# First stage of a state-space block written out as a four-deep pipeline, and its skip term moved to the third stage

## The chip, the cores and the metric

The kernel runs on one core of a Trainium2 chip. Its engines are TensorE (PE in the profile; PEld is its weight load), VectorE (DVE), ScalarE (ACT), GpSimd (POOL) and SyncE (SP, which here only starts transfers). The metric is the device time of one execution in microseconds (us); lower is better.

## The reference, cut to what matters

The input `x` holds 2 x 4096 tokens of 512 numbers. Four layers follow each other, each added to `x`; the change touches only the first one:

```python
xin = layernorm(x)                      # what the layer gets
xn = layernorm(xin) * norm_w + norm_b   # a second norm inside the layer
proj = xn @ x_proj_w.T                  # 128 + 64 + 64 columns
delta, B, C = split(proj)
dt = softplus(delta @ dt_proj_w.T + dt_proj_b)
h = exp(dt * A) * h + dt * B * xn       # a scan over the tokens, 512 x 64 states
y = sum_n h * C
out = (y + xin * D_param) @ out_proj_w.T
```

The skip term is `xin * D_param`: the once-normed input times a row of 512 constants. C is taken from the first 128 tokens of a sequence.

## The kernel before, in words

The 8192 tokens are cut into NCH = 16 chunks of T = 512. P is 128 (partitions), Q = 4 blocks of 128 columns, J = 4 blocks of 128 tokens. The program has five stages, one after the other, each with its own buffers; between two stages all engines and transfers finish. Everything is in 32-bit floats. Every engine runs its own list of instructions in order, and semaphores (`wait_ge`, `then_inc`) hold one behind another. A `Count` is a semaphore whose value encodes chunk and step.

**First stage (`pre_phase`).** For each chunk: load x (SP), statistics and both norms `z` and `zh` (DVE, with a power on POOL for the root), transposes of `zh` and of `z` (PE, `work`, L357), `znt` out of PSUM with scale and bias (ACT, L312), `zt` out of PSUM (DVE, L282), projection with `xp` (PE, L367), copies `dl` and `bc` (DVE), the step sizes with `dtw` (PE, L372), `xb` out of PSUM with a bias (ACT, L315), Abs, Exp and Ln (ACT, L333 to L335), `dt` and `v` (DVE, L293, L294), transposes of `bc` and `v` (PE, `turn_rows`, L381, L387), copies into rows (ACT, L322, L325), and stores of `zt`, `bc`, `dt`, `br` and `vr`. A chunk owns one half of PSUM (four banks of `tp`), which its steps use one after another. `skewed` runs pieces marked 1 for chunk c + 1 and pieces marked 0 for chunk c in one turn. On ACT the order is

```python
skewed(act, NCH, [(1, columns), (0, rows), (1, exponents)])
```

**Scan (`scan_phase`).** For each chunk and each of 128 items (pairs of states by column blocks), PE makes the input u (L602, `inputs`), ACT the decay, DVE the scan (L663), POOL multiplies by C (L489), and PE transposes and adds the product into `y_ps` (L610, `reduce`). An item's `inputs(i)` is followed in PE's list by `reduce(i - 3)`. At item 3 of a chunk PE first waits until ACT has copied the last chunk's y out of PSUM (L528), and then starts y with the skip term: 16 products of `z` with the diagonal `dd` (L622), which take 32 matmul records. Only then come `reduce(0)` and `inputs(4)`.

**Third stage (`mid_phase`).** For each chunk: transposes of y (PE, `turn_y`, L896 with `mid_yr`), the output projection (L890), a sum and a norm (DVE), a second product (L908), its sum and norm, and four projections of the normed rows (L919, L944). The last of these, `values`, has one DVE copy (L817) for each of its four PSUM banks. The orders are

```python
skewed(dve, NCH, [(1, first_sum), (1, second_sum), (0, keys), (1, more_norms), (0, values)])
skewed(pe, NCH, [(1, turn_y), (0, decay), (1, attn_out), ..., (0, values_early), (1, turn_xn), (0, values_late)])
```

so PE's `turn_y` of the next chunk stands right behind `values_late` of this one.

Of the kernel before, what the change touches and what calls it, by code (L numbers as in the profile page):

```python
# [3 lines left out]
ALU = mybir.AluOpType  # L4
# [3 lines left out]
P = 128  # L8
T = 512
# [134 lines left out]
NORM_BOTH = 10  # L144
# [16 lines left out]
def both_norms(dve, cnt, roots, item, root_n, outs, x, mv, ve, r0, rr, tmp, tiles):  # L161

    roots.wait(dve, item, root_n)
    cnt.link(dve, dve.tensor_tensor(tmp, r0, r0, ALU.mult))
    cnt.link(dve, dve.tensor_tensor(tmp, tmp, ve, ALU.mult))
    cnt.link(dve, dve.tensor_scalar(tmp, tmp, -0.5, 1.5, ALU.mult, ALU.add))
    cnt.link(dve, dve.tensor_tensor(rr, r0, tmp, ALU.mult))
    for e in (1, 0):
        for j in range(tiles):
            last = dve.tensor_scalar(outs[e][:, j, :], x[:, j, :], mv[:, j, 0:1], rr[:, e, j:j + 1], ALU.subtract, ALU.mult)  # L170
        cnt.inc(last)


# [6 lines left out]
def pre_phase(nc, NCH, D, x_d, xp_d, dtw_d, nw_d, nb_d, dtb_d, ident_d, dt_s, vr_s, z_s, bc_s, br_s):  # L180

# [3 lines left out]
    J = T // P  # L187
    with ExitStack() as ctx:
# [3 lines left out]
        tp = ps("tp", [P, 2, Q, T])  # L192
        x = sb("x", [P, 2, J, D]); z = sb("z", [P, 2, J, D]); zh = sb("zh", [P, 2, J, D])
        zt = sb("zt", [P, 2, Q, T]); znt = sb("znt", [P, 2, Q, T])
        dl = sb("dl", [P, T]); bc = sb("bc", [P, 2, T])
        xb = sb("xb", [P, 2, Q, T]); ab = sb("ab", [P, 2, Q, T]); dt = sb("dt", [P, 2, Q, T]); v = sb("v", [P, 2, Q, T])
        vr = sb("vr", [P, J, D]); br = sb("br", [P, J, P])
        st = sb("st", [P, J, 6]); mv = sb("mv", [P, J, 2]); ve = sb("ve", [P, 2, J])
        half_neg = sb("half_neg", [P, 2, J]); r0 = sb("r0", [P, 2, J]); rr = sb("rr", [P, 2, J]); tmp = sb("tmp", [P, 2, J])
# [23 lines left out]

        @block.sync
        def _(sp):
            for dst, src in ((xp, xp_d), (dtw, dtw_d), (ident, ident_d), (nw, nw_d), (nb, nb_d), (dtb, dtb_d)):
                sp.dma_start(dst[:], src).then_inc(consts, 16)

            for par in range(2):
                sp.sem_inc(outs[par], 48)  # L230

            def load(c, par, half):

                norm_steps.wait_freed(sp, c)
                sp.dma_start(x[:, par], xv[c]).then_inc(x_in[par], 16)

            def store(c, par, half):

                proj_steps.wait(sp, c, Q + 2)
                sp.dma_start(z_s[c], zt[:, par]).then_inc(outs[par], 16)  # L240
                sp.dma_start(bc_s[c], bc[:, par]).then_inc(outs[par], 16)
                proj_steps.wait(sp, c, Q + 3)
                sp.dma_start(dt_s[c], dt[:, par]).then_inc(outs[par], 16)
            staggered(sp, NCH, [(2, load), (0, store)])
            for par in range(2):
                sp.wait_ge(outs[par], 48 * (NCH // 2 + 1))

        @block.gpsimd
        def _(pool):
# [3 lines left out]

            def roots(c, par, half):
                root_steps.begin(c)
                root_pool(pool, root_steps, norm_steps, c, BOTH_VE, r0[:], ve[:], half_neg[:])
            in_turn(pool, NCH, roots)

        @block.vector
        def _(dve):  # L260
            norm_steps.start(dve)
            proj_steps.start(dve)

            def stats(c, par, half):
                norm_steps.begin(c)
                dve.wait_ge(x_in[par], (half + 1) * 16)
                both_stats(dve, ticks_dve, norm_steps, x[:, par], st, mv, ve, J)

            def norms(c, par, half):

                pe_steps.wait_freed(dve, c)
                both_norms(dve, norm_steps, root_steps, c, 1, (z[:, par], zh[:, par]), x[:, par], mv, ve[:], r0[:], rr[:], tmp[:], J)

            def turned(c, par, half):
                proj_steps.begin(c)

                dve.wait_ge(outs[par], (half + 1) * 48)

                row_turns.wait_freed(dve, c)
                pe_steps.wait(dve, c, 2)  # L280
                for q in range(Q):
                    proj_steps.inc(dve.tensor_copy(zt[:, par, q, :], tp[:, par, q, :]))  # L282

            def copies(c, par, half):
                pe_steps.wait(dve, c, 3)
                proj_steps.inc(dve.tensor_copy(dl[:], tp[:, par, 0, :]))
                pe_steps.wait(dve, c, 4)
                proj_steps.inc(dve.tensor_copy(bc[:, par, :], tp[:, par, 1, :]))
# [1487 lines left out]
```

## Time and profile before

| what | us |
|---|---|
| median of 3 runs (lowest, highest) | 8550.32 (8546.56, 8552.54) |
| the profiled execution, its own time | 8550.57 |
| its span, first to last instruction | 8548.7 |
| first stage | 0 to 578.6 |
| scan | 578.6 to 5455.7 |
| third stage | 5455.7 to 6962.3 |
| fourth and fifth stage | 6962.3 to 8548.7 |

A row of a timeline gives the start, the length and what ran; equal neighbours are merged (x16), and the bracket at its end is the time for which the engine sat idle before. The stage bounds are the first start of a transfer of the next stage's constants.

### The profile page before, as it was taken

What the parts mean: (1) busy time and instruction counts of PE and PEld (TensorE: products, weight loads), DVE (VectorE), ACT (ScalarE), POOL (GpSimd) and SP (SyncE); (2) the same over time, 40 slices, a digit from 0 to 9 for tenths busy, and PEclk for the clock granted to TensorE, in tenths of its full rate; (3) what the DMA queues carried; (4) which work ended last, traced back from release to release, by engine and by line L of the source; (5) the groups of instructions that cost most, each with busy time, mean ns of one, the idle gap of its engine ahead of it and who ended that gap; (6) DMA issues with size and microseconds to landing.
All of it is one profiled execution on the core that took longest, in us unless ns stands there. A gap on an engine that the chain in (4) does not pass through costs nothing. (4 is left out here: it accounts for less than half of the span.)

```text
span 8548.7 us, 222310 instructions
## 1 busy us (share of the span) xinstructions
PE 7615.9 (89%) x76550; PEld 5597.7 (65%) x76550; DVE 6621.9 (77%) x8318; ACT 4693.7 (55%) x10584; POOL 5667.3 (66%) x3272
## 2 busy tenths in 40 slices
PE   5669999999999999999999999799999989999984
PEld 3347777777777777777777777544444446666653
DVE  4459999999999999999999999522222247787866
ACT  4457777777777777777787777411111112222220
POOL 0019999999999999999999999500000025545444
PEclk8779999999999999999999999999999988888885
DMA  3350000000000000000000000112212122222225
GB/s 130 138 157 9 21 21 1 20 21 20 0 21 21 0 21 21 15 6 21 21 0 21 21 0 5 75 69 88 83 69 88 74 89 77 76 76 78 75 67 168
DMA packets 198856, 423.21 MB, mean 50 GB/s; under 512 B 22544, under 2 KB 48592, under 8 KB 183120
## 3 DMA queue, kind: packets, MB, share of 16 engines
q1 hardware_dynamic: 172864, 382.77, 13.4%
q10 hardware_dynamic: 25872, 38.80, 1.3%
q8 instruction: 80, 1.31, 0.1%
q14 instruction: 40, 0.33, 0.0%
HBM read 225.11 MB, written 196.41 MB: 49 GB/s over the span
## 5 line engine op out<-in xcount | busy, mean ns | idle before, releaser
L489 POOL TENSOR_TENSOR scan_hc<-scan_h,scan_cb 128x1024 f32<-128x1024 f32 x2048 | 4775.4, 2367 | 165.4 <-DVE scan_h L663 96.7
L663 DVE TENSOR_TENSOR_SCAN scan_h<-scan_a,scan_carry,scan_u 128x512 f32<-128x512 f32 x4096 | 4800.3, 1255 | 56.1 <-POOL scan_hc L489 48.8
L548 ACT ACTIVATE scan_a<-scan_dt,scan_aneg 128x512 f32<-128x512 f32 x4096 | 2658.1, 708 | 7.3 <-ACT scan_yo L528 7.3
L602 PE MATMUL scan_u<-scan_dg,scan_v 64*128 64x128 f32 x32768 | 2379.8, 285 | 308.7 <-DVE scan_h L663 265.1
L602 PEld LDWEIGHTS scan_u<-scan_dg,scan_v 64*128 64x128 f32 x32768 | 1990.4, 187 | 786.8 <-DVE scan_h L663 549.5
L610 PE MATMUL scan_y<-scan_ident,scan_hc 128*128 128x128 f32 x16408 | 2239.9, 279 | 7.0 <-POOL scan_hc L489 3.1
L610 PEld LDWEIGHTS scan_y<-scan_ident,scan_hc 128*128 128x128 f32 x16408 | 1756.9, 140 | 256.3 <-POOL scan_hc L489 14.2
L519 ACT ACTIVATE scan_dg<-scan_half,scan_bt 128x64 f32<-128x64 f32 x4096 | 1139.1, 341 | 5.3 <-DVE scan_onward L646 5.2
L177 POOL TENSOR_TENSOR mid_r<-mid_ve,mid_half_neg 128x4 f32<-128x4 f32 x32 | 32.4, 1012 | 1271.3 <-DVE mid_ve L132 784.1
L540 ACT ACTIVATE scan_carry<-scan_h,scan_onward 128x4 f32 (+1 forms) x1008 | 303.0, 301 | 979.1 <-DVE scan_h L663 979.1
L1153 POOL TENSOR_TENSOR core_joint<-core_own 128x32 f32<-128x32 f32 x64 | 17.4, 272 | 621.2 <-DVE core_own L1283 564.0
L800 DVE TENSOR_TENSOR mid_x<-mid_x,mid_pa 128x512 f32<-128x512 f32 x64 | 44.1, 689 | 429.8 <-PE mid_pa L908 429.8
L855 ACT ACTIVATE mid_rt<-mid_pb 128x512 f32<-128x512 f32 x64 | 38.2, 597 | 610.1 <-PE mid_pb L919 610.1
L1355 ACT COPY core_ats<-core_at_ps 128x512 f32<-128x512 f32 x128 | 68.7, 589 | 549.0 <-PE core_at_ps L1422 549.0
L177 POOL TENSOR_TENSOR pre_r<-pre_ve,pre_half_neg 128x8 f32<-128x8 f32 x16 | 26.3, 1642 | 479.7 <-DVE pre_ve L158 479.7
L789 DVE TENSOR_TENSOR mid_x<-mid_x,mid_pa 128x512 f32<-128x512 f32 x64 | 43.9, 686 | 355.4 <-PE mid_pa L890 355.4
L1497 PE MATMUL core_y_ps<-core_wo,core_ot 128*128 128x512 f32 x512 | 301.2, 743 | 0.0
L817 DVE COPY mid_vv<-mid_pb 128x512 f32<-128x512 f32 x64 | 44.3, 692 | 306.0 <-PE mid_pb L944 306.0
L1280 DVE TENSOR_TENSOR core_rk<-core_rr,core_k 128x128 f32<-128x128 f32 (+7 forms) x512 | 267.7, 523 | 0.0
L919 PE MATMUL mid_pb<-mid_xnt,mid_wr 128*128 128x512 f32 x512 | 223.9, 595 | 20.7 <-DVE mid_kt L812 20.7
L850 ACT ACTIVATE mid_at<-mid_pb,mid_bwn 128x512 f32<-128x512 f32 x64 | 43.9, 687 | 344.4 <-PE mid_pb L919 319.9
L1278 DVE TENSOR_TENSOR core_rr<-core_rr,core_a 128x128 f32<-128x128 f32 (+6 forms) x448 | 219.3, 490 | 9.4 <-PE core_at_ps L1422 8.6
(211 smaller groups left out, 7651.8 us busy)
## 6 DMA issues: line engine op xcount, KB each, us to landing
scratch_y<-scan_yo ACTq DMA_DIRECT2D x17, 1024.0 KB, 4.4
pre_x<-in_x SPq DMA_DIRECT2D x16, 1024.0 KB, 6.7
scratch_z<-pre_zt SPq DMA_DIRECT2D x16, 1024.0 KB, 3.9
scratch_dt<-pre_dt SPq DMA_DIRECT2D x16, 1024.0 KB, 4.6
scratch_vr<-pre_vr ACTq DMA_DIRECT2D x16, 1024.0 KB, 4.7
scan_dt<-scratch_dt SPq DMA_DIRECT2D x16, 1024.0 KB, 5.2
scan_v<-scratch_vr SPq DMA_DIRECT2D x32, 512.0 KB, 7.6
scan_z<-scratch_z SPq DMA_DIRECT2D x16, 1024.0 KB, 9.8
```

The costliest lines, as they stand in the source:

```text
L489: pool.tensor_tensor(hc[:, q].rearrange("p n (r j) -> p n r j", j=P), h[:, q].rearrange("p n (r j) -> p n r j", j=P), cb[:, bass.ds(b * NS ...
L519: last = act.activation(dg[:, buf, k, :, n], half[:], ACT.Identity, scale=bt[:, par, k, bass.ds(first + n, 1)])
L540: act.activation(carry[:, q0:q0 + 2, bass.ds(first, 2)], h[:, q0:q0 + 2, :, T - 1], ACT.Identity, scale=keep[:, bass.ds(c, 1)]).then_inc(s ...
L548: ins = act.activation(a[:, q, n, :], dt[:, par, q, :], ACT.Exp, scale=aneg[:, q, bass.ds(m * 2 + n, 1)])
L602: mm = pe.matmul(u_ps[:, q % 2, g, k * HP:(k + 1) * HP, :], v[row, par, k, q, :], dg[row, buf, k], start=True, stop=True)
L610: mm = pe.matmul(y_ps[:, j, q * P:(q + 1) * P], hc[:, q, n, j * P:(j + 1) * P], ident[:], is_transpose=True, start=False, stop=True, skip_ ...
L663: ins = dve.tensor_tensor_scan(h[:, q, n, :], a[:, q, n, :], u_ps[:, q % 2, :, :, n].rearrange("p g t -> p (g t)"), carry[:, q, bass.ds(m ...
L919: mm = pe.matmul(pb[:, o, :], weight[:, q, o * P:(o + 1) * P], src[:, q, :], start=(q == 0), stop=(q == Q - 1))
L1278: decayed = chain.inc(dve.tensor_tensor((rr[:, j - 1] if j else first[:, par])[:, j:W], rr[:, j, j:W], a[:, par, j:j + 1, :].broadcast_to( ...
L1280: chain.inc(dve.tensor_tensor(rk[:, par, j:W, j, :], rr[:, j, j:W], k[:, par, j:j + 1, :].broadcast_to(shape), ALU.mult))
L1355: act_a.inc(act.copy(ats[:, h2], at_ps[:, h2]))
L1497: mm = pe.matmul(y_ps[:], ot[:, q, :], wo[:, q, :], start=(q == 0), stop=(q == Q - 1))
```

## The change

The first stage no longer loops: `unrolled` writes its 16 chunks out, each piece with its own lead (up to 3 chunks on DVE, 5 for the loads). PSUM is split by use: four banks `ta_ps` for the transposes of `zh` and the step sizes, two `xb_ps` for the projection, two `row_ps` for the rows. `z`, its norm, its transposes, `zt` and its store are gone; the mean and the factor of each token go out in one small store, `scale_s`. The Abs on ACT becomes a DVE instruction, `fold` (the smaller of x and -x), so that Exp needs no sign change. All transfers start on SP. In the scan the load of `z`, the diagonal and the 16 products are gone; `reduce(0)` of a chunk starts the sums itself, bank by bank behind ACT's copies. In the third stage a DVE piece `skips` with a lead of 2 makes `(x - mean) * skip`, then adds its product with the factor to y: eight 128 x 512 instructions in two groups of four. PE's `turn_y` waits for it. `scale` is loaded with y, and `skip` is an eleventh constant.

```diff
+def unrolled(items, pieces):
+    deep = max(lead for lead, _ in pieces)
+    for turn in range(-deep, items):
+        for lead, piece in pieces:
+            if 0 <= turn + lead < items:
+                piece(turn + lead)
...
-        tp = ps("tp", [P, 2, Q, T])
+        ta_ps = ps("ta_ps", [P, Q, T]); xb_ps = ps("xb_ps", [P, 2, T]); row_ps = ps("row_ps", [P, 2, T])
...
+            load(0)
+            for dst, src in ((ident, ident_d), (nw, nw_d), (nb, nb_d), (xp, xp_d), (dtw, dtw_d), (dtb, dtb_d)):
+                sp.dma_start(dst[:], src).then_inc(consts, 16)
+            unrolled(NCH, [(1, store_bc), (0, store_dt), (0, store_rows), (5, lambda c: c and load(c))])
+            norm_steps.wait_all(sp, NCH - 1)
+            sp.dma_start(scale_s.rearrange("c p n -> p c n"), scale[:]).then_inc(scale_out, 16)
...
+            def softplus(c):
+                exps.wait_all(dve, c)
...
+                if c:
+                    dve.wait_ge(row_turned, c * ROWS)
+                dve.tensor_tensor(v[:], dt[:, c % 2], znt[:, c % 3], ALU.mult).then_inc(v_ready, 1)
+            def fold(c):
+                dve.wait_ge(xb_ready, (c + 1) * Q)
+                dve.scalar_tensor_tensor(out=ab[:], in0=xb[:, c % 2], scalar=-1.0, in1=xb[:, c % 2], op0=ALU.mult, op1=ALU.min).then_inc(folded, 1)
...
-            skewed(dve, NCH, [(0, turned), (1, stats), (0, copies), (1, norms), (0, softplus)])
+            unrolled(NCH, [(1, copy_bc), (0, softplus), (1, fold), (3, stats), (2, copy_dl), (3, norm)])
...
+            def rows(c):
+                if c >= 2:
+                    act.wait_ge(rows_out[c % 2], (c // 2) * 32)
+                for k in range(ROWS):
+                    act.wait_ge(row_turned, c * ROWS + k + 1)
+                    src = row_ps[:, (c * ROWS + k) % 2]
+                    act.copy(vr[:, c % 2, k - 1, :] if k else br[:, c % 2].rearrange("p j n -> p (j n)"), src).then_inc(row_copied, 1)
...
-            skewed(act, NCH, [(1, columns), (0, rows), (1, exponents)])
+            unrolled(NCH, [(1, biased), (2, columns), (0, rows), (1, exponents)])
...
+            def turn_rows(c):
+                pe.wait_ge(bc_ready, c + 1)
+                for k in range(ROWS):
+                    if c * ROWS + k >= 2:
+                        pe.wait_ge(row_copied, c * ROWS + k - 1)
+                    if k == 1:
+                        pe.wait_ge(v_ready, c + 1)
...
-            skewed(pe, NCH, [(1, work), (0, turn_rows)])
+            unrolled(NCH, [(1, steps), (2, turn_zh), (0, turn_rows), (2, project)])
...
-                reduce(c * PER + m * Q + q - 3, (q + 1) % Q)
+                reduce(c * PER + m * Q + q - 3, (q + 1) % Q, q == 3 and isinstance(m, int) and m == 0)
...
+                            if first and n == 0:
+                                pe.wait_ge(y_copied, c * K + j + 1)
...
+            def skips(c, par, half):
+                dve.wait_ge(y_in[par], (half + 1) * 32)
+                dve.wait_ge(x_in[par], (half + 1) * 16)
+                for j in range(J):
+                    last = dve.scalar_tensor_tensor(out=h[:, j, :], in0=x[:, par, j, :], scalar=scale[:, par, 2 * J + 2 * j:2 * J + 2 * j + 1], in1=skip[:], op0=ALU.subtract, op1=ALU.mult)
+                last.then_inc(scaled, 1)
+                dve.wait_ge(scaled, c + 1)
+                for j in range(J):
+                    last = dve.scalar_tensor_tensor(out=yr[:, par, j, :], in0=h[:, j, :], scalar=scale[:, par, j:j + 1], in1=yr[:, par, j, :], op0=ALU.mult, op1=ALU.add)
+                last.then_inc(skipped, 1)
...
-            skewed(dve, NCH, [(1, first_sum), (1, second_sum), (0, keys), (1, more_norms), (0, values)])
+            dve.wait_ge(consts, CONSTS * 16)
+            staggered(dve, NCH, [(1, first_sum), (1, second_sum), (0, keys), (1, more_norms), (0, values), (2, skips)])
...
-                pe.wait_ge(y_in[par], (half + 1) * 16)
+                pe.wait_ge(skipped, c + 1)
```

## Rows read from the trace of the kernel before

**Rows 1.** Busy time by stretch; columns: stretch, length, PE, PEld, DVE, ACT, POOL, clock, DMA, GB/s:
```profile
0.00:578.60 578.60, 342.42 (x1216) 204.48 (x1216) 251.18 (x480) 258.93 (x288) 26.56 (x21) 0.77 0.36 132
578.60:5455.70 4877.10, 4539.50 (x49696) 3806.64 (x49696) 4808.48 (x4107) 3848.68 (x9287) 4775.42 (x2048) 1.00 0.06 16
5455.70:6962.30 1506.60, 1432.31 (x3872) 673.65 (x3872) 348.56 (x800) 212.34 (x336) 104.85 (x49) 0.99 0.22 83
```

**Rows 2.** All instructions of one line on `pre_xb`, with first and last start:
```profile
L293 DVE SCALAR_TENSOR_TENSOR pre_dt<-pre_xb,pre_ab x16: 2291/2293/2293, 52.8 to 563.0; 128x2048 f32<-128x2048 f32 x16
```

**Rows 3.** Timeline of one chunk of the first stage: start, length, engine, line, [idle before]:
```profile
307.84 3.70 PE L372 MATMUL pre_tp<-pre_dl,pre_dtw 128*128 128x512 f32 x8 [0.78 <-DVE pre_bc L288]
...
311.81 1.91 PE L387 MATMUL pre_tp<-pre_ident,pre_v 128*128 128x128 f32 x16
...
312.63 2.06 ACT L325 COPY pre_vr<-pre_tp 128x512 f32<-128x512 f32 x4
...
314.82 1.96 PE L357 MATMUL pre_tp<-pre_ident,pre_zh 128*128 128x128 f32 x16 [1.10 <-ACT pre_vr L325]
...
317.83 1.28 ACT L334 ACT_TABLE_LOAD   x1
...
319.12 1.91 ACT L334 ACTIVATE pre_ab<-pre_ab 128x2048 f32<-128x2048 f32 x1
...
324.16 2.77 ACT L312 ACTIVATE pre_znt<-pre_tp,pre_nb,pre_nw 128x512 f32<-128x512 f32 x4
...
324.97 3.67 PE L357 MATMUL pre_tp<-pre_ident,pre_z 128*128 128x128 f32 x16 [8.20 <-ACT pre_znt L312]
...
331.35 5.49 PE L367 MATMUL pre_tp<-pre_znt,pre_xp 128*128 128x512 f32 x6 [2.71 <-DVE pre_zt L282]
```

**Rows 4.** Busy time in stretches of one us, columns as in the first group:
```profile
315.00:316.00 1.00, 1.00 (x11) 1.00 (x11) 0.00 (x0) 0.10 (x1) 0.00 (x0) 1.00 0.20 60
319.00:320.00 1.00, 0.00 (x0) 0.00 (x0) 0.00 (x0) 0.99 (x2) 0.00 (x0) 0.88 0.42 158
336.00:337.00 1.00, 1.00 (x2) 0.41 (x2) 0.00 (x0) 0.00 (x0) 0.20 (x1) 0.58 0.00 0
```

**Rows 5.** Timeline, start and end of the first stage:
```profile
10.25 2.47 DVE L151 BATCH_NORM_STATS2 pre_st<-pre_x 128x6 f32<-128x512 f32 x4 [10.25 <-DMA pre_x<-in_x]
...
16.22 1.92 DVE L170 TENSOR_SCALAR pre_zh<-pre_x,pre_mv,pre_rr 128x512 f32<-128x512 f32 x4
...
573.37 0.53 ACTq L328 DMA_DIRECT2D scratch_vr<-pre_vr  x1
```

**Rows 6.** Timeline, one chunk boundary of the scan:
```profile
904.73 2.02 ACT L528 COPY scan_yo<-scan_y 128x512 f32<-128x512 f32 x4
...
905.44 3.81 PE L622 MATMUL scan_y<-scan_dd,scan_z 128*128 128x128 f32 x32 [0.30 <-ACT scan_yo L528]
...
910.05 1.16 PE L602 MATMUL scan_u<-scan_dg,scan_v 64*128 64x128 f32 x16
...
911.65 14.17 DVE L663 TENSOR_TENSOR_SCAN scan_h<-scan_a,scan_carry,scan_u 128x512 f32<-128x512 f32 x12 [3.05 <-POOL scan_hc L489]
```

**Rows 7.** Timeline, one turn boundary of the third stage:
```profile
6169.69 7.03 PE L944 MATMUL mid_pb<-mid_wv,mid_xnt 128*128 128x512 f32 x16
...
6176.56 1.91 PE L896 MATMUL mid_pa<-mid_ident,mid_yr 128*128 128x128 f32 x16
6176.76 0.69 DVE L817 COPY mid_vv<-mid_pb 128x512 f32<-128x512 f32 x1 [2.74 <-PE mid_pb L944]
```

**Rows 8.** Timeline, start of the third stage:
```profile
5465.37 7.48 SPq L737 DMA_DIRECT2D mid_x<-in_x  x1
...
5481.08 1.96 PE L896 MATMUL mid_pa<-mid_ident,mid_yr 128*128 128x128 f32 x16 [2.02 <-ACT mid_wxw L829]
```

**Rows 9.** All transfers into `mid_x` and `scratch_x`, from issue to landing:
```profile
DMA to landing us min/median/max: 4.3/5.9/17.8
```

More of the change, by code:

```diff
@@ L237, in store @@
[L237 to L246, printed above, removed]
+                sp.wait_ge(dt_out[par], 16 * (NCH // 2))
@@ L252, in _ @@
             pool.wait_ge(half_ready, 1)
-            def roots(c, par, half):
+            for c in range(NCH):
                 root_steps.begin(c)
                 root_pool(pool, root_steps, norm_steps, c, BOTH_VE, r0[:], ve[:], half_neg[:])
-            in_turn(pool, NCH, roots)
         @block.vector
@@ L274, in turned @@
[L274 to L288, printed above, removed]
@@ L330, in exponents, with biased @@
[L330 to L337 removed]
+            def biased(c):
+                if c >= 2:
+                    act.wait_ge(dt_ready, c - 1)
+                for q in range(Q):
+                    act.wait_ge(steps_made, c * Q + q + 1)
+                    act.activation(xb[:, c % 2, q, :], ta_ps[:, q], ACT.Identity, bias=dtb[:, q:q + 1]).then_inc(xb_ready, 1)
@@ L389, in _, with steps, turn_zh @@
-            skewed(pe, NCH, [(1, work), (0, turn_rows)])
-def scan_phase(nc, B, L, a_log, d_diag, ident_d, half_ident_d, dt_s, vr_s, z_s, bc_s, br_s, y_s):
+            def steps(c):
+                pe.wait_ge(dl_ready, c + 1)
+                pe.wait_ge(columns_ready, (c + 1) * Q)
+                for q in range(Q):
+                    pe.matmul(ta_ps[:, q], dtw[:, q * P:(q + 1) * P], dl[:], start=True, stop=True).then_inc(steps_made, 1)
+            def turn_zh(c):
+                norm_steps.wait_all(pe, c)
+                for q in range(Q):
+                    if c:
+                        pe.wait_ge(xb_ready, (c - 1) * Q + q + 1)
+                    for j in range(J):
+                        mm = pe.transpose(ta_ps[:, q, j * P:(j + 1) * P], zh[:, j, q * P:(q + 1) * P], ident[:])
+                    mm.then_inc(zh_turned, 1)
@@ new lines, in turn_rows @@
+            def turn_rows(c):
[5 more added lines that the diff above has]
+                        pe.wait_ge(v_ready, c + 1)
+                    for n in range(J if k == 0 else Q):
+                        src = v[:, n, (k - 1) * P:k * P] if k else bc[:, c % 2, n * P:(n + 1) * P]
+                        mm = pe.transpose(row_ps[:, (c * ROWS + k) % 2, n * P:(n + 1) * P], src, ident[:])
+                    mm.then_inc(row_turned, 1)
@@ new lines, in project @@
+            def project(c):
+                for i in range(2):
+                    if c:
+                        pe.wait_ge(bc_ready if i else dl_ready, c)
+                    for q in range(Q):
+                        if i == 0:
+                            pe.wait_ge(columns_ready, c * Q + q + 1)
+                        mm = pe.matmul(xb_ps[:, i], xp[:, q, i * P:(i + 1) * P], znt[:, c % 3, q, :], start=(q == 0), stop=(q == Q - 1))
+                    mm.then_inc(projected, 1)
+            unrolled(NCH, [(1, steps), (2, turn_zh), (0, turn_rows), (2, project)])
@@ L603, in inputs, with reduce @@
                     mm.then_inc(u_ready, 1)
-                def reduce(i, q):
+                def reduce(i, q, first=False):
                     pe.wait_ge(hc_ready, i + Q + 1)
@@ L1693, in program @@
     x_rows = x.rearrange("b l d -> (b l) d")
-    dt_s, z_s = (scratch(n, by_column) for n in ("dt", "z"))
+    dt_s = scratch("dt", by_column)
+    scale_s = scratch("scale", [NCH, P, 4 * T // P])
     vr_s = scratch("vr", [N, D])
```

242 lines of the change are left out of this document (107 added, 135 removed).

## The prediction

> **What bounds the kernel now.** I read the busy time by stretch first, cut at the stage bounds. The scan has 57% of the span, and there DVE is busy for 4808.5 of 4877.1 us: it is bound by DVE. The third stage is bound by PE, 1432.3 of 1506.6 us. The first stage, 578.6 us, is bound by no engine: PE has 342.4, DVE 251.2, ACT 258.9, and the granted clock is 0.77 [rows 1]. The fourth and fifth stage are not touched. Next I took one line of the first stage that runs once per chunk: its first and last start, 52.8 and 563.0, give (563.0 - 52.8)/15 = 34.0 us per chunk [rows 2]. The timeline of one such chunk shows why: PE stands idle for 8.2 us behind ACT's Exp and Ln and then runs its transposes in 3.67 us where 1.96 were enough before, because its clock fell in the pause; then it waits 2.7 us more for DVE's copies [rows 3]. The work is a chain through three engines, hardly overlapped. So each of the three stages must be costed by its own limit.
>
> **First stage: the work of a turn.** Prices are those at the full clock. PE: step sizes 8 records of 0.43, 3.5 us (3.70 with the last one's tail); transposes of `zh` 1.96; rows 20 transposes at 1.91/16 = 0.12, 2.4 [rows 3]; projection 16 records, as long as 16 of the same form in the third stage, 6.9 between starts [rows 7]. Sum 14.7. ACT: `znt` 2.77, `xb` as much, five copies near 2.06 x 5/4 = 2.6, Exp and Ln 1.91 each with a table load of 1.28 each [rows 3], 6.4. Sum 14.5; the Abs (1.91, by the Exp row) is gone. DVE: three instructions over 2048 columns, `fold` being the new one and of the form of L293, 3 x 2.29 = 6.9 [rows 2]; statistics 2.47 and `zh` 1.92 [rows 5]; two copies of 0.69 [rows 7]; and small ones. The way from statistics to `zh` is 5.97, so what is not statistics in it is at most 3.5 [rows 5]. Sum at most 16.2. Three engines, 14.5 to 16.2 us each. Gone from DVE are the norm `z` and four copies.
>
> **How they interlock.** Let a turn start at 0 with PE's step sizes of chunk t+1. They end at 3.4; ACT takes `xb` behind them bank by bank, to 4.5. PE turns `zh` of t+2 to 5.4; ACT takes `znt` to 7.2. PE turns the `bc` rows to 5.9 and the first `v` row by 6.4, if DVE has `v` by then: DVE has copied `bc` (1.0) and run its two softplus instructions (5.6), just in time. Then PE stalls: `row_ps` has two banks, and ACT comes to the first row copy only at 7.2. From there PE and ACT alternate, and PE's last row is issued near 9.7. Projection runs from 9.7 to 16.6. That is the next turn's start, since the copy of `dl` waits only for the first half of it (13.2, done 14.0). ACT: row copies to 10.5, Exp and Ln to 16.9, and its next wait ends only 1.16 after PE's start. DVE: `fold` to 7.9, statistics to 11.2, `dl` to 14.0, norm to about 16.9. So PE closes the loop, with 14.7 of work and 1.9 of stall; ACT and DVE are within half a us. With handshakes I take 16.9 us. The other buffers (`dt`, `bc`, rows double, `znt` triple) are released at least a turn earlier. Transfers: 3.5 MB per turn, and landing times under 10 us [rows 9] lie beside two turns of cover; on SP's queue, a load stands behind the row store and waits for the norm at the turn's end, but it has over 20 us before its use.
>
> **Filling and draining.** x of chunk 0 is now issued first, about 3 us earlier than it was for 10.25 [rows 5]: statistics at 7, `zh` at 14.6, first products at half clock; `steps` of chunk 0 near 26 and turn 0 near 38.5. Turn 14 then starts at 38.5 + 14 x 16.9 = 275. Chunk 15 has nothing beside it: step sizes, `fold` to +8, Exp and Ln behind the rows of 14 to +15, softplus +19.6, rows at half clock +24. The old stage ended 5.2 us after the row store was issued at 573.37 [rows 1, 5]; the new one has the store of `scale` behind it, 2048 pieces of 64 bytes, whose price no row has. Between 0 (it lies beside the row store) and 14 I take 2.5. End: 275 + 31 = 306, a gain of 272. Bounds: a turn of 16.6 and a quick fill -285; a turn of 20 (below) and a slow end -215.
>
> **The clock in the new turns.** The pause of PE in a turn is 1.9 us in parts, but between step sizes and projection lie 6.2 us of transposes and stalls. The rows speak for the full clock: at 315, where PE had run only transposes since 307.84 + 3.70 = 311.5, it is 1.00 and stays so until the stretch at 319, whose 0.88 puts the fall at 319.8, 3.0 us after the last transpose ended (316.8) and 8.2 after the last product [rows 3, 4]. I charge nothing, and keep 14 x 3 = 40 us as the bound.
>
> The Trainium skill ("TensorE: Matmul & The Clock Gate", Part 4) says that transposes do not count as activity for the clock. By it those 6.2 us would be a pause that drops the clock each turn. This trace's stretch at 315, with eleven transposes and no product at 1.00, speaks against it, though 8.2 us is all that it covers.
>
> **Scan.** The waits name POOL for DVE's 3.05 us, once per chunk, but POOL's product had ended before; what ends at the right time is PE's `inputs(4)`, 910.05 + 1.16 = 911.21, 0.44 before DVE starts [rows 6]. It was late because L622 takes 3.81. Without it `reduce(0)` starts its banks behind ACT's copies, 905.44 to about 906.9, four more transposes to 907.5; `inputs(4)` ends 908.7, DVE starts at 909.15, where it could have at 908.6. The stall is 0.6 for 3.05: 16 x 2.45 = 39. ACT's next decay is ready at nearly the same time, so no more is to be had. With the diagonal gone from the start, 1 us more. Together 40; bounds 25 and 50 (the whole stall and the start).
>
> **Third stage.** `skips` of chunk t+2 stands last in DVE's turn, behind the four copies of `values`, and PE's next turn begins with `turn_y` of t+2, which waits for it. Before, `turn_y` starts at 6176.56 straight behind the products; the last copy runs 6176.76 to 6177.45 [rows 7]. Then come eight instructions with two operands of 512 columns: a quarter of 2.29 is 0.57 [rows 2], 0.69 for a lone one [rows 7], so 0.6 each in a run, 4.8, and 0.1 between the groups and at the end. PE starts at 6182.4: 5.9 us late, and nothing hides it, since PE has no pause before L896 and everything behind it in its list is held too. It happens for chunks 2 to 15: 14 x 5.9 = 82. Bounds per turn 5.3 and 6.3, from 0.54 and 0.65 each. On top, the clock. In the rows it fell 3.0 us into the pause of 8.2 [rows 3, 4]; a pause of 5.7 is nearly twice as long, so it will mostly fall, if not each time at the same delay. It came back in the stretch at 336, whose 0.58 means 336.8, 5.5 us after the products resumed at 331.35 [rows 3, 4]. That is 2.7 us lost when it falls; I take 1.9 a turn, seven falls in ten: 14 x 1.9 = 27 (bounds 0 and 38). Start: `turn_y` of chunk 0 ran at 5481.08, but x, issued at 5465.37, lands up to 17.8 later, 5483.2 [rows 8, 9], 0.6 more behind `skip`; then 4.9 of `skips`: 5488.8, 7.8 late, and turned at half clock, 1.7 more [rows 3]. Chunk 1's `skips` lie under PE's wait for ACT there. Together 82 + 27 + 9.5 = 118; bounds 85 and 140.
>
> **Sum.** -272 - 40 + 118 = -194. The profiled execution took 8550.57, 0.25 above the median of the runs shown, so its time serves for both: 8550.6 - 194 = 8356.6, say 8357.
>
> **Rivals.**
> (a) As above, within 8325 to 8395: 0.62.
> (b) The first stage's turns are 19 to 22 us: the clock falls in each between step sizes and projection, 2.7 a turn, 8395; or DVE, whose sum may be 16.2, and ACT trade small waits with PE. For it: all three are within 2 us of each other. Against: the stretch at 315. 14 x 2.5 to 14 x 5 more, 8392 to 8427: 0.14, of which half for the clock. The rule of the Trainium skill named above would give this case.
> (c) The third stage loses more: 10 us a turn or more instead of 7.8, as the transposes behind the pause put off the clock's return, from 8357 + 31 = 8388 to 8430: 0.07.
> (d) The clock holds through the third stage's pause and the first stage runs at its floor: 8357 - 27 - 13 = 8317, down to 8300: 0.08.
> (e) PE stays at half clock in the first stage: 2 x 14.7 = 29.4 a turn, 12.5 more, 8532, with fill 8545, no difference. Against: dense products brought the clock back after 5.5 us [rows 4]. 0.03.
> (f) Slower. The chain through PE, ACT and DVE stays closed in each turn as it is now: if `v` of chunk t needs its Exp and Ln from the same turn, projection stands behind `turn_rows` in PE's list and waits with it, and a turn stays at 34.0 [rows 2]: 14 x 17.1 = 239 more, 8596. It decides from a turn of 16.9 + 194/14 = 30.8 us on. This is also the case that the pipeline does nothing. Against: the leads give Exp and Ln to the turn before. 0.06.
>
> **How the numbers follow.** A measurement of this kernel tells 0.2% (17 us) from no change. (a) to (d) are faster, 0.91; (e) is the same, with a rest of (f), 0.03; the rest slower, 0.06. The range takes the bounds of the three terms without all of them at one end, 8310 to 8435: it leaves out (e), (f) and the tails, some 0.16.
>
> **What would show it.** In the profile after: the first stage ends near 306, its L293 successor has a step near 17 us, PE's clock is near 1.00 in it and PE idles before the row transposes behind ACT's row copies. In the scan DVE's stall per chunk is near 0.6 and the span of the stage 40 shorter. In the third stage PE waits 14 times some 5.8 us for DVE's `skips`, with a clock below 1.00 behind it. The prediction is wrong if the turn is not PE's (ACT's or DVE's list without a pause), if `skips` takes less than 0.55 an instruction, or if an unrolled list costs PE pauses that no row here has.

## The result and the profile after

The changed kernel takes 8358.83 us (median of 4 runs, 8355.94 to 8361.57) against 8550.91 for the kernel before (4 runs, 8546.56 to 8552.54). The ratio is 0.9779, with a 95% interval from 0.9767 to 0.9791: faster by 2.2%. The forecast was 8357. The profiled execution of the changed kernel has a span of 8359.7 us, 189.0 less than before, and this difference can be split at the stage bounds:

| stage | before | after | difference | forecast |
|---|---|---|---|---|
| first | 578.6 | 297.6 | -281.0 | -272 |
| scan | 4877.1 | 4835.0 | -42.1 | -40 |
| third | 1506.6 | 1642.6 | +136.0 | +118 |
| fourth and fifth | 1586.4 | 1584.5 | -1.9 | 0 |
| span | 8548.7 | 8359.7 | -189.0 | -194 |

Busy time by stretch, cut at the new stage bounds, with the columns of [rows 1]:

```profile
0.00:297.60 297.60, 241.47 (x960) 138.30 (x960) 217.34 (x368) 231.18 (x272) 26.53 (x21) 0.96 0.58 201
297.60:5132.60 4835.00, 4491.25 (x49184) 3750.12 (x49184) 4807.59 (x4103) 3851.78 (x9287) 4776.00 (x2048) 1.00 0.05 13
5132.60:6775.20 1642.60, 1470.62 (x3872) 702.01 (x3872) 434.82 (x928) 212.49 (x336) 104.83 (x49) 0.95 0.20 77
```

Set it beside [rows 1]. In the first stage PE, DVE and ACT are each busy for over 217 of 297.6 us, where before they had at most 342 of 579: PE's busy time fell by 101 us, DVE's and ACT's by 34 and 28, and the stage by 281: most of it went out of the gaps, not out of the work. In the scan DVE has the same 4808 us of work, with 27 us beside it instead of 69. In the third stage PE's busy time rose by 38 us although its 3872 instructions are the same, and the clock fell from 0.99 to 0.95.

**First stage.** The line that answers to [rows 2]:

```profile
L287 DVE SCALAR_TENSOR_TENSOR pre_dt<-pre_xb,pre_ab x16: 2276/2281/2291, 40.9 to 281.3; 128x2048 f32<-128x2048 f32 x16
```

The step is (281.3 - 40.9)/15 = 16.03 us where it was 34.0. Its last interval holds part of the drain; PE's own turns, from turn 0 at 37.91 to the last step sizes at 265.61, are 227.7/14 = 16.26 us. One turn in the timeline, to be read against [rows 3]:

```profile
152.10 3.60 PE L364 MATMUL pre_ta_ps<-pre_dl,pre_dtw 128*128 128x512 f32 x8
...
155.53 1.91 PE L372 MATMUL pre_ta_ps<-pre_ident,pre_zh 128*128 128x128 f32 x16
...
156.32 2.77 ACT L339 ACTIVATE pre_znt<-pre_ta_ps,pre_nb,pre_nw 128x512 f32<-128x512 f32 x4
...
158.97 0.60 ACT L347 COPY pre_br<-pre_row_ps 128x512 f32<-128x512 f32 x1
...
159.62 1.14 PE L384 MATMUL pre_row_ps<-pre_ident,pre_v 128*128 128x128 f32 x8 [1.31 <-ACT pre_br L347]
...
160.95 0.66 PE L384 MATMUL pre_row_ps<-pre_ident,pre_v 128*128 128x128 f32 x4 [0.19 <-ACT pre_vr L347]
161.44 7.03 PE L394 MATMUL pre_xb_ps<-pre_znt,pre_xp 128*128 128x512 f32 x16
...
165.08 0.69 DVE L306 COPY pre_dl<-pre_xb_ps 128x512 f32<-128x512 f32 x1 [2.18 <-PE pre_xb_ps L394]
```

The pause of 8.20 us behind ACT is gone. What is left of PE's idle time is 1.31 + 0.19 = 1.50 us, behind ACT's row copies and nothing else: `row_ps` has two banks, ACT comes to the first copy only after `znt`, and this is the place that the prediction named. PE's transposes of `zh` take 1.91, so the clock is up. Busy time in the steady part of the stage:

```profile
60.00:252.00 192.00, 174.23 (x705) 98.58 (x704) 160.57 (x276) 170.91 (x201) 19.63 (x12) 1.00 0.63 222
```

PE is busy for 174 of 192 us and the granted clock is 1.00. The end of the stage, to be read against [rows 5]:

```profile
290.83 0.51 SPq L249 DMA_DIRECT2D scratch_vr<-pre_vr  x1
291.39 0.55 SPq L256 DMA_DIRECT2D scratch_scale<-pre_scale  x1
297.63 0.35 SPq L454 DMA_DIRECT2D scan_alog<-in_a_log  x1
```

From the row store's issue to the next stage it is 6.80 us, against 5.2 before. I put the 1.6 us between them down to the store in small pieces (forecast 2.5); no run takes that store away alone.

**Scan.** One chunk boundary, to be read against [rows 6]:

```profile
620.05 2.02 ACT L533 COPY scan_yo<-scan_y 128x512 f32<-128x512 f32 x4
620.75 0.72 PE L617 MATMUL scan_y<-scan_ident,scan_hc 128*128 128x128 f32 x2 [0.29 <-ACT scan_yo L533]
...
622.12 0.77 PE L617 MATMUL scan_y<-scan_ident,scan_hc 128*128 128x128 f32 x5 [0.16 <-ACT scan_yo L533]
...
622.81 1.16 PE L606 MATMUL scan_u<-scan_dg,scan_v 64*128 64x128 f32 x16
...
624.41 2.45 DVE L659 TENSOR_TENSOR_SCAN scan_h<-scan_a,scan_carry,scan_u 128x512 f32<-128x512 f32 x2 [0.48 <-POOL scan_hc L494]
```

`reduce(0)` starts its banks right behind ACT's copies, `inputs(4)` ends at 622.81 + 1.16 = 623.97, and DVE stalls for 0.48 us instead of 3.05. Over the stage these stalls are 7.8 us in 16 times.

**Third stage.** PE's transposes of y and DVE's skip instructions in the steady part (chunks 2 to 15), by line, and then who waited for DVE's:

```profile
L906 PE MATMUL mid_pa<-mid_ident,mid_yr x224: 421/421/473, 5333.5 to 6624.1; 128*128 128x128 f32 x112
L789 DVE SCALAR_TENSOR_TENSOR mid_yr<-mid_h,mid_scale,mid_yr x56: 745/746/752, 5330.6 to 6620.0; 128x512 f32<-128x512 f32 x56
...
PE mid_pa L906: 87.9, 14
```

PE waited 14 times, 6.28 us each. No transpose of y in these 14 turns ran at the full clock: the shortest took as long as the median, 421 ns, where those of skips_early below take 273. One turn boundary, DVE's and PE's rows, to be read against [rows 7]:

```profile
5427.39 2.73 DVE L785 SCALAR_TENSOR_TENSOR mid_h<-mid_x,mid_scale,mid_skip 128x512 f32<-128x512 f32 x4
5430.15 2.74 DVE L789 SCALAR_TENSOR_TENSOR mid_yr<-mid_h,mid_scale,mid_yr 128x512 f32<-128x512 f32 x4
...
5433.02 3.67 PE L906 MATMUL mid_pa<-mid_ident,mid_yr 128*128 128x128 f32 x16 [6.28 <-DVE mid_yr L789]
```

And the clock around it, in stretches of one us:

```profile
5429.00:5430.00 1.00, 0.00 (x0) 0.00 (x0) 1.00 (x2) 0.00 (x0) 0.00 (x0) 1.00 1.03 385
5430.00:5431.00 1.00, 0.00 (x0) 0.00 (x0) 0.96 (x3) 0.00 (x0) 0.00 (x0) 0.67 1.05 297
...
5436.00:5437.00 1.00, 1.00 (x5) 0.82 (x4) 0.00 (x0) 0.27 (x1) 0.00 (x0) 0.50 1.05 408
5437.00:5438.00 1.00, 1.00 (x3) 0.38 (x2) 0.00 (x0) 1.00 (x3) 0.00 (x0) 0.91 0.44 164
```

The products before ended at 5433.02 - 6.28 = 5426.74. A stretch of 0.67 between 1.00 and 0.50 puts the fall at 5430.3, 3.6 us into the pause; one of 0.91 puts the return at 5437.2, 4.2 us after PE resumed. So PE works 4.2 us at half clock in this turn, and 4.1 in two others (those of 5730.04 and 6323.95, where the clock returns at 5734.1 and 6328.1). The start of the stage, to be read against [rows 8]:

```profile
5161.42 2.74 DVE L785 SCALAR_TENSOR_TENSOR mid_h<-mid_x,mid_scale,mid_skip 128x512 f32<-128x512 f32 x4 [39.38 <-DMA mid_x<-in_x]
...
5167.19 3.65 PE L906 MATMUL mid_pa<-mid_ident,mid_yr 128*128 128x128 f32 x16 [11.36 <-DVE mid_yr L789]
...
5172.99 15.70 PE L900 MATMUL mid_pa<-mid_wout,mid_yt 128*128 128x512 f32 x32 [2.14 <-ACT mid_yt L846]
...
5202.35 17.03 PE L918 MATMUL mid_pa<-mid_w,mid_ht 128*128 128x512 f32 x32 [2.14 <-ACT mid_ht L852]
```

and the first of the two products in the kernel before:

```profile
5485.19 14.00 PE L890 MATMUL mid_pa<-mid_wout,mid_yt 128*128 128x512 f32 x32 [2.14 <-ACT mid_yt L836]
```

`turn_y` of chunk 0 starts 34.6 us after the stage, where it was 25.4 (+9.2), and takes 3.65 instead of 1.96 (+1.7). The two products of chunk 0 take 15.70 and 17.03 us where both took 14.00 before (+1.7 and +3.0). In the first the clock is 1.00 when it starts, falls at 5174.3 and is back at 5177.8; the second starts at 0.50 and gets the full clock only at 5208.5, while the second product of the kernel before started at 1.00. Together these put `turn_y` of chunk 1 15.6 us later than before, counted from the start of the stage.

### The profile page after: what moved, and what is told of

It reads as the page before. It is cut to its first block and busy times, and to the rows that moved or that the text cites. A ratio compares the mean times of both kernels' runs of the same rounds, so it can differ in the third digit from the quotient of the medians.

```text
span 8359.7 us, 220056 instructions
## 1 busy us (share of the span) xinstructions
PE 7512.8 (90%) x75782; PEld 5505.6 (66%) x75782; DVE 6668.3 (80%) x8330; ACT 4668.4 (56%) x10568; POOL 5670.6 (68%) x3272
## 5 line engine op out<-in xcount | busy, mean ns | idle before, releaser
L929 PE MATMUL mid_pb<-mid_xnt,mid_wxw 128*128 128x512 f32 x512 | 230.6, 604 | 0.9 <-DVE mid_vv L826 0.9
L918 PE MATMUL mid_pa<-mid_w,mid_ht 128*128 128x512 f32 x512 | 225.5, 599 | 2.1 <-ACT mid_ht L852 2.1
```

The source lines that it names most:

```text
L918: mm = pe.matmul(pa[:, j, :], ht[:, q, j * P:(j + 1) * P], w["w0"][:, q, :], start=(q == 0), stop=(q == Q - 1))
L929: mm = pe.matmul(pb[:, o, :], weight[:, q, o * P:(o + 1) * P], src[:, q, :], start=(q == 0), stop=(q == Q - 1))
```

## The experiments

Eight kernels ran. The kernel before, on the same chip as these, had a median of 8543.59 us (13 runs, 8538.16 to 8551.21). Where one time stands without a range (busy_pause, half_skips, two_deep, before_no_z, abs_on_act) the kernel was timed once, and I read the lengths of its stages and turns in the trace rather than its total. "Less" and "later" are against the changed kernel's profiled execution, except in the two kernels that start from the one before.

### The skip instructions one place earlier in DVE's list

```diff
-            staggered(dve, NCH, [(1, first_sum), (1, second_sum), (0, keys), (1, more_norms), (0, values), (2, skips)])
+            staggered(dve, NCH, [(1, first_sum), (1, second_sum), (0, keys), (1, more_norms), (2, skips), (0, values)])
```

> The changed kernel with one edit: in DVE's list of the third stage the piece skips stands before values, in DVE's pause of 8.8 us, and not behind it. Theory: the cost of the moved skip term is PE's pause behind skips and the clock that falls in it, 14 x (6.3 + 2.3) = 119 us; both vanish, PE never waits for skips in the steady part, and the time is 8359 - 119 = 8240. Rival: eight more DVE instructions (5.5 us a turn) cost about the same wherever they stand, since they push values or the norms: the gain is below 40 us, 8320 or more.

Measured: 8238.67 us (8237.85 to 8242.46), ratio to the kernel before 0.9642 (0.9626 to 0.9658). The third stage is 1524.3 us, 118.3 less than in the changed kernel. DVE now runs the eight instructions while PE is in the projections, and `turn_y` has no wait in front of it; PE's transposes of y in two turns:

```profile
5418.56 1.91 PE L906 MATMUL mid_pa<-mid_ident,mid_yr 128*128 128x128 f32 x16
5509.05 1.91 PE L906 MATMUL mid_pa<-mid_ident,mid_yr 128*128 128x128 f32 x16
```

Their distance is 90.5 us, that of the kernel before (6267.06 - 6176.56), where the changed kernel has 99.0. So the skip term costs the steady third stage only by its place in the list: neither DVE's eight instructions nor the extra load of `scale` costs PE anything when they lie beside its products. Of the 1524.3 - 1506.6 = 17.7 us that stay, 17.3 are there when `turn_y` of chunk 2 starts (195.2 us after the start of the stage, against 177.9 before): they belong to the start.

### PE kept busy in the pause

```diff
-                pe.wait_ge(skipped, c + 1)
                 turn_steps.wait_before(pe, c)
+                for k in range(44):
+                    pe.transpose(pa[:, k % Q, 0:P], ident[:], ident[:])
+                pe.wait_ge(skipped, c + 1)
                 turn(yr[:, par])
```

> The changed kernel, but in the third stage PE runs 44 extra transposes of the identity (5.3 us at the full clock) into a free PSUM bank before it waits for skips; nothing else is changed and the pause itself stays. Theory: transposes alone hold the clock, so the transposes of y take 1.9 us instead of 3.65 and the first products behind them are at 2.4 GHz; the turn is 2.2 us shorter, the time 8359 - 31 = 8328. Rival, the rule of the Trainium skill (TensorE: Matmul & The Clock Gate, Part 4) that transposes do not count as activity: the clock falls as before and the time stays at 8359.

Measured: 8338.25 us; the third stage is 1615.5, 27.1 less. Timeline, then the clock in the stretch behind the remaining wait:

```profile
5427.08 4.97 PE L892 MATMUL mid_pa<-mid_ident 128*128 128x128 f32 x44
...
5433.45 1.97 PE L907 MATMUL mid_pa<-mid_ident,mid_yr 128*128 128x128 f32 x16 [1.40 <-DVE mid_yr L789]
```

```profile
5434.00:5435.00 1.00, 1.00 (x11) 1.00 (x10) 0.00 (x0) 0.00 (x0) 0.00 (x0) 1.00 1.05 365
```

PE starts `turn_y` as late as before, but at the full clock. The turn is 96.9 us instead of 99.0, and this difference is all clock. From the end of the last product, at about 5427, to the next one, at 5435.26, PE runs only transposes for 8 us, with one wait of 1.40, and the clock is 1.00 to the end; it is 1.00 from 5400 to 6600 as a whole, where the changed kernel has 0.97. The 14 turns give 14 x 2.1 = 29 us, and the extra transposes cost 2 in the first two turns; I had expected 31. The Trainium skill ("TensorE: Matmul & The Clock Gate", Part 4) says, beside figures for bf16, that transposes do not count as activity for the clock; by it this kernel would gain nothing. For these transposes in 32 bits the run contradicts it.

### A pause about half as long

```diff
                 dve.wait_ge(scaled, c + 1)
-                for j in range(J):
-                    last = dve.scalar_tensor_tensor(out=yr[:, par, j, :], in0=h[:, j, :], scalar=scale[:, par, j:j + 1], in1=yr[:, par, j, :], op0=ALU.mult, op1=ALU.add)
-                last.then_inc(skipped, 1)
+                dve.sem_inc(skipped, 1)
```

> The changed kernel without the second group of four instructions in skips, so the skip term is computed and never added to y. PE's pause shrinks from 6.3 to about 3.5 us. Theory A: the clock falls about 3 us into a pause, as it did in the 8.2 us pause of the kernel before, so nearly every turn still loses 2.2 us: 14 x 2.8 = 39 less, 8320. Theory B: a pause of 3.5 us is mostly survived; the clock's part goes too, 14 x (2.8 + 2.2) = 70 less, 8290.

Measured: 8315.83 us; the third stage is 1595.3, 47.3 less. Timeline of one boundary and the clock in three stretches:

```profile
5425.48 3.58 PE L904 MATMUL mid_pa<-mid_ident,mid_yr 128*128 128x128 f32 x16 [3.57 <-DVEq L788]
```

```profile
5424.00:5425.00 1.00, 0.00 (x0) 0.00 (x0) 1.00 (x2) 0.00 (x0) 0.00 (x0) 1.00 1.01 385
5425.00:5426.00 1.00, 0.52 (x3) 0.52 (x4) 0.29 (x1) 0.00 (x0) 0.00 (x0) 0.81 1.07 336
5426.00:5427.00 1.00, 1.00 (x7) 1.00 (x6) 0.00 (x0) 0.00 (x0) 0.00 (x0) 0.50 0.94 182
```

The pause is 6.28 - 3.57 = 2.71 us shorter, 38 us in 14 turns. But the clock still falls, at 5425.6, when PE has already resumed 0.1 us ago; the transposes then take 2.75 to 3.67 us in the steady turns, against 1.91 at the full clock. From the first to the last steady `turn_y` a turn is 95.9 us, 3.1 less than in the changed kernel: 2.7 of it are the wait, and 0.4 of the clock's 2.2 come back. Half of the skip work saves nearly half of the wait and little of the clock's part, which is my theory A; the rest of the 47.3 us lies in the first turns.

### Two chunks deep instead of four

```diff
-            unrolled(NCH, [(1, copy_bc), (0, softplus), (1, fold), (3, stats), (2, copy_dl), (3, norm)])
+            unrolled(NCH, [(0, softplus), (1, copy_dl), (1, copy_bc), (1, fold), (2, stats), (2, norm)])
...
-            unrolled(NCH, [(1, biased), (2, columns), (0, rows), (1, exponents)])
+            unrolled(NCH, [(1, columns), (1, biased), (0, rows), (1, exponents)])
...
-            unrolled(NCH, [(1, steps), (2, turn_zh), (0, turn_rows), (2, project)])
+            unrolled(NCH, [(1, turn_zh), (1, project), (1, steps), (0, turn_rows)])
```

The loads have a lead of 4 instead of 5.

> The changed kernel with the first stage two deep instead of four: PE runs turn_zh, project and steps of chunk t+1 and then turn_rows of t; ACT columns and biased of t+1, rows of t, exponents of t+1; DVE softplus of t, the copies and fold of t+1, statistics and norm of t+2. Same instructions, same buffers. Theory: depth is what pays; ACT's columns, PE's projection and step sizes, ACT's biased, rows and exponents then stand in one loop of about 22.5 us a turn against 16.1: 14 x 6.4 = 90 more, 8450. Rival: the gain came from the PSUM banks by use and the work that left, and depth adds nothing: 8360 to 8375.

Measured: 8497.45 us. The step of `softplus` is (414.6 - 39.3)/15 = 25.0 us, and the stage ends at 431.0, 133.4 later. Timeline and clock of one turn:

```profile
164.91 3.67 PE L372 MATMUL pre_ta_ps<-pre_ident,pre_zh 128*128 128x128 f32 x16 [7.52 <-DVE pre_zh L317]
```

```profile
160.00:161.00 1.00, 0.00 (x0) 0.00 (x0) 0.34 (x4) 1.00 (x1) 0.55 (x1) 1.00 0.98 373
162.00:163.00 1.00, 0.00 (x0) 0.00 (x0) 0.73 (x5) 0.99 (x2) 0.09 (x1) 0.50 0.79 291
```

PE waits 7.52 us for DVE's `zh`, which lies behind the statistics of the same turn; the clock falls in this pause, and the transposes take 3.67 instead of 1.91. These 1.8 us are most of the 2.5 by which the turn exceeds what I expected; the rest I have not attributed. The depth pays: with the same instructions, fewer chunks in flight (PE and ACT span two instead of three), and the order that goes with it, a turn is 9.0 us longer. Depth and order were not parted.

### The kernel before without the transposes of z

Edit, in the kernel before: the norm into `z`, its transposes, the four copies into `zt` and the store of `zt` are taken out of the first stage, and the scan loads the array of step sizes in the place of `z`, so that its products stay.

> The kernel before with only the work on z taken out of its first stage: no norm z, no transposes of z, no copies zt, no store of it; projection waits for the columns alone. The scan loads dt in the place of z, so the skip term is wrong and the transfer stays. Theory: of the 281 us that the first stage gained, the work that left is the small part: the loop loses the 3.7 us of transposes and the 2.7 us wait for the copies, gives back about 1, so a turn is 34.0 - 5 = 29, 80 us less, 8470; the other 200 us are overlap. Rival: the work that left is most of the gain, 8350 or less.

Measured: 8468.54 us. The step is (481.6 - 46.3)/15 = 29.0 us instead of 34.0, and the stage ends at 496.6, 82.0 earlier. Of the 281.0 us of the first stage, less work alone gives 82. The other 199 come with the rest of the change, and the end of the stage in two_deep splits them: 496.6 - 431.0 = 66 with the PSUM banks by use, the buffers, the new order, the earlier first load, the transfers on SP and the Abs on DVE together, which no run parts further but for the Abs below, and 133 with the depth and its order. In the three kernels with the loop, the two-deep and the four-deep order, the step goes 29.0, 25.0, 16.0.

### In the kernel before, inputs(4) ahead of the 16 products

```diff
                     for q in range(Q):
-                        inputs(m, q, buf)
+                        if not (q == 0 and isinstance(m, int) and m == 1):
+                            inputs(m, q, buf)
                         if q == 3 and isinstance(m, int) and m == 0:
+                            inputs(1, 0, 1)
```

> The kernel before with one edit in the scan: at each chunk boundary PE issues inputs(4) before the products of the skip term instead of behind them and reduce(0). Theory: DVE's stall of 3.05 us per chunk is PE's late inputs(4), whatever releaser the profile names; now inputs(5) is the late one, DVE's stall is about 1.9 us and the scan 16 x 1.15 = 18 us shorter, 8533. Rival: POOL, which the profile names, is the cause: the stall stays 3.05 and the time 8551.

Measured: 8553.04 us, ratio 1.001 (1.000 to 1.002): no gain, as the rival said. But the timeline shows a stall that has moved, not one that POOL holds:

```profile
894.70 12.98 DVE L665 TENSOR_TENSOR_SCAN scan_h<-scan_a,scan_carry,scan_u 128x512 f32<-128x512 f32 x11
...
905.40 0.97 PEld L602 LDWEIGHTS scan_u<-scan_dg,scan_v 64*128 64x128 f32 x16 [1.37 <-DVE scan_h L665]
...
906.49 3.84 PE L624 MATMUL scan_y<-scan_dd,scan_z 128*128 128x128 f32 x32
908.12 2.45 DVE L665 TENSOR_TENSOR_SCAN scan_h<-scan_a,scan_carry,scan_u 128x512 f32<-128x512 f32 x2 [0.43 <-POOL scan_hc L489]
...
910.17 1.91 PE L610 MATMUL scan_y<-scan_ident,scan_hc 128*128 128x128 f32 x16
...
912.01 1.16 PE L602 MATMUL scan_u<-scan_dg,scan_v 64*128 64x128 f32 x16
...
913.10 1.09 PE L610 MATMUL scan_y<-scan_ident,scan_hc 128*128 128x128 f32 x8
913.48 7.14 DVE L665 TENSOR_TENSOR_SCAN scan_h<-scan_a,scan_carry,scan_u 128x512 f32<-128x512 f32 x6 [2.90 <-PE scan_u L602]
```

At item 4 the stall named POOL shrinks from 3.05 to 0.43 us, so the cause of the old one was PE's list and not POOL. Then the same time comes back one item later, 2.90 us, and now under PE's name: the 3.84 us of products stand in front of `inputs(5)`. My error was to take them as late for one item only. Per item PE has 1.16 + 1.09 = 2.25 us of `inputs` and `reduce`, and DVE two scans of 12.98/11, 2.36 us. PE gains 0.1 us an item on DVE, so it cannot make up 3.8 us of products before DVE has used its lead. Of the two ways tried, only taking the products away, as the change does, gives the time back.

### The Abs back on ACT

```diff
+                act.wait_ge(xb_ready, (c + 1) * Q)
+                if c:
+                    act.wait_ge(dt_ready, c)
+                exps.link(act, act.activation(ab[:], xb[:, c % 2], ACT.Abs))
+                exps.link(act, act.activation(ab[:], ab[:], ACT.Exp, scale=-1.0))
-                act.wait_ge(folded, c + 1)
-                exps.link(act, act.activation(ab[:], ab[:], ACT.Exp))
```

`fold` is gone from DVE's list.

> The changed kernel with Abs back on ACT in front of Exp and the DVE instruction fold gone. Theory: DVE has slack of over 2 us in a turn and ACT nearly none (its list has 14.5 us of work in a turn of 16.1 and waits only 0.8 for the first step sizes), so 1.9 us more on ACT make a turn about 1.3 to 1.8 us longer and 2.3 us less on DVE give nothing: 14 x 1.5 = 21 more, 8380. Rival: DVE closes the loop, and the turn gets shorter: 8340.

Measured: 8359.37 us. The step is (285.1 - 38.8)/15 = 16.4 us, 0.4 longer, and the stage ends at 301.4, 3.8 later. The 1.91 us of the Abs cost ACT 0.4, as ACT had waits of some 1.6 us in a turn (0.76 for the first step sizes, the others 0.17 to 0.26); so ACT does not close the loop of the changed kernel. DVE's list was 2.28 us shorter in this run and the turn no shorter; with the 2.18 us for which DVE waits for PE in the turn shown above, this leaves PE, with its 1.50 us behind the row copies. In this run ACT has no wait for the step sizes any more: its list of 14.4 + 1.9 = 16.3 us has become the turn, and it closes the loop here. (That DVE would close the loop of the changed kernel at just 16.0 us is not excluded by this run alone; its waits are what speaks against it.) My size was wrong: moving the Abs is worth 4 us in this stage, not 20, and nothing that shows in the total.

### Early skips, inputs(4) ahead and the first loads in front

It puts together the early skips, `inputs(4)` ahead in the scan, and the loads of chunk 0 of the third stage in front of the five weights that it doesn't need yet:

```diff
+            sp.dma_start(yr[:, 0], yv[1]).then_inc(y_in[0], 16)
+            sp.dma_start(scale[:, 0], scale_s[0]).then_inc(y_in[0], 16)
+            sp.dma_start(x[:, 0], xv[0]).then_inc(x_in[0], 16)
+            sp.dma_start(skip[:], skip_d.partition_broadcast(P)).then_inc(skip_in, 16)
             loads = [(w["wout"]
```

> The changed kernel with skips before values as in skips_early, with inputs(4) of the scan issued ahead of reduce(0) at each chunk boundary, and with y, scale, x of chunk 0 and skip loaded in the third stage before the five weights that come later (skip on a semaphore of its own). Theory: against skips_early the rest of the stall per chunk in the scan goes, 16 x 0.5 = 8, and the third stage's first turn_y starts 5 to 7 us earlier and at the full clock: 14 to 17 us below skips_early, 8225. Rival: the reordered loads delay the weights by as much as they bring y forward, and ACT, not PE, holds DVE in the scan: equal to skips_early, 8240.

Measured: 8238.02 us (8237.31 to 8240.55), ratio 0.9641 (0.9625 to 0.9657): no different from skips_early, which is what the rival said and not the 8225 of the theory. The third stage is 1520.6, 3.7 shorter: the first skips are done at 5152.8, but `turn_y` of chunk 0 then waits for ACT's copy of `wxw`, which stands behind the transfer of `bw`, one of the last constants. It starts 3.8 us sooner in the stage, and at half clock still (3.68 us). The scan is 4835.7, unchanged. Its boundary shows why:

```profile
621.69 1.16 PE L606 MATMUL scan_u<-scan_dg,scan_v 64*128 64x128 f32 x16 [1.18 <-DVE scan_h L662]
622.59 2.56 ACT L553 ACTIVATE scan_a<-scan_dt,scan_aneg 128x512 f32<-128x512 f32 x4 [0.46 <-ACT scan_yo L533]
...
624.41 4.79 DVE L662 TENSOR_TENSOR_SCAN scan_h<-scan_a,scan_carry,scan_u 128x512 f32<-128x512 f32 x4 [0.43 <-POOL scan_hc L494]
```

Here `inputs(4)` ends at 622.85, over 1.5 us before DVE starts, and DVE starts at 624.41 all the same, 0.43 us after its last scan. So the last 0.4 us per chunk is not PE's. The row names POOL, but POOL doesn't fit: item 4 waits only for POOL's product of item 0 (`hc_ready`), which ended near 619.6, and at the first boundary of this run DVE starts at 323.97, in the middle of a product on POOL. What fits is ACT, whose decay of item 4 stands behind its copies of y: the second Exp of x4 ends at about 623.91, 0.50 before DVE starts, and at the first boundary, where the row does name ACT's decay, it is 0.50 as well (323.47 to 323.97). In the changed kernel PE's `inputs(4)`, 0.44 before DVE, and this decay, 0.56 before it, end nearly together. No run moved ACT's copies, so that ACT is the cause is argued and not shown.

## Why the prediction was right, step by step

The forecast (a) came true, in time (8358.83 for 8357) and in mechanism. The terms, by its own steps:

- **The work of a turn and how it interlocks.** Right. PE's work in a turn is 16.21 - 1.50 = 14.71 us (forecast 14.7), and its stall lies behind ACT's row copies, 1.50 for 1.9. ACT's work is 14.4 (14.5), DVE's 13.6, where the forecast had only a bound, 16.2. The landing times, put there at under 10 us, reach 17.8 in [rows 9]; it did not matter, as nothing in the steady turns waits for a transfer. The 0.3 that I added for handshakes was not paid, and the stall is 0.4 shorter: a turn of 16.26 for 16.9, 14 x 0.64 = 9 us better, which is the whole of the term's error. That ACT does not close the loop was only argued; abs_on_act shows it, and DVE's wait of 2.18 us for PE speaks against DVE, without a run of its own.
- **Filling and draining.** Turn 0 started at 37.9 (38.5), the end came 32.0 after the last step sizes (31).
- **The clock in the new turns.** Right at nothing: it is 1.00 over 192 us, with some 6 us of transposes and short stalls in every turn, and busy_pause shows by an edit that transposes alone hold it. Rival (b) is out, with the step of 16 us and with the rule on which its clock half rests.
- **Scan.** Right, 42.1 for 40, and so is the reading that the releaser in the profile, POOL, was not the one. The stall left is 0.48 for 0.6. The remark that ACT's next decay is ready at nearly the same time, so that no more is to be had, agrees with the last run, where `inputs(4)` ended over 1.5 us before DVE's start and DVE started no sooner.
- **Third stage, the pause.** The place is right, the price too low: 6.28 for 5.9. The eight instructions took 2.73 + 2.74 = 5.47 us, 0.68 each in a run, where I took 0.6 between a quarter of 2.29 and a lone copy of 0.69; the steps around them took 0.81 for 1.1.
- **Third stage, the clock.** The step that was off: "seven falls in ten" and 2.7 us for each. It fell in all 14 turns, and each fall cost 99.0 - 90.5 - 6.28 = 2.2 us. The two errors pull against each other, 2.2 a turn for 1.9. Together with the pause 14 x 8.5 = 119 for 109.
- **Third stage, the start.** 16.7 for 9.5, the largest error of a term against its size. The 7.8 us by which `turn_y(0)` was to be late were 9.2, and its transposes at half clock cost the 1.7 that I had. What I left out is that the clock's trouble goes on behind them: 1.7 and 3.0 us in the two products of chunk 0, and 1.1 up to the place where `turn_y` of chunk 2 would start.

Of the rivals, (c) shares the direction, as the loss in a turn was 8.5 and not 7.8, but it stays under its 10; (d) is ruled out, as the clock fell each time, (e) and (f) by the step of 16 us. The three errors, -9, -2 and +18 us, and -2 in the untouched stages, nearly cancel; the total was closer than its terms.

What the change leaves behind is larger than any of these errors: 118 of the 136 us that the third stage lost were a matter of one place in DVE's list.

## What to carry to other kernels

When work moves to another stage, place it in the list by who waits for it: an operation whose result the bounding engine needs at the start of its next turn (here `skips`) belongs ahead of those that follow this turn's last products (here the copies of `values`), and the test is whether the bounding engine has a wait in front of it. In this kernel that one place was worth 118 us. A pause of the bounding engine costs its length and then the clock's part as well, so a short stall in dense work is dearer than its row of waits says. When a stall is to be taken away by a new order, check how much slack the engine has over the following items; without it the stall only moves on, and the profile then names it differently.

## What the runs showed of the hardware that I had not expected

- Transposes of 128 x 128 in 32 bits alone held TensorE's clock at 2.4 GHz: 1.00 over the 8 us between products in busy_pause (with one wait of 1.40), where the same stretch left idle brings it to 0.50 (1.2 GHz).
- They can also bring it back. In the changed kernel the transposes from 5167.19 to 5170.84 are all that PE did since 5155.83, and the clock is back at 5170.9, 2 us before the next product; the same happened in the kernel before, where the clock was back at 5511.4 after transposes from 5507.04 to 5510.71, with the next product at 5512.86. In skips_early and in the last run the same transposes at the same place were not enough, and it returned 5.9 us after the products started.
- The fall does not come at one fixed delay. The clock fell 3.6 us (changed kernel) and 3.7 us (half_skips) after the last product in the turns shown, though in the second PE had just resumed, where the prediction read 3.0 us; at the start of the third stage of the changed kernel it is 4.9 us (5155.8 to 5160.7) and then 2.7 (5188.7 to 5191.4), and in the kernel before 5.4 (5499.2 to 5504.6). It came back 4.2 us after PE resumed with transposes and then products, sooner than the 5.5 us that the prediction read in the first stage of the kernel before, and 6.1 after the second product of chunk 0 started (5202.35 to 5208.5).
- A `scalar_tensor_tensor` over 128 x 512 with a scalar per partition is recorded at 0.745 us and takes 0.68 in a run of four; the form over 128 x 2048 with a constant takes 2.28, 0.57 per 512 columns.
